# Residuals on TensorE, full-turn row transposes and a partition-aligned split in a decoder kernel

## The reference

```
x = layernorm(x + gated_delta_attention(x))        # stage 1
x = layernorm(x + cross_attention(x, ctx))         # stage 2
x = layernorm(x + quantum_ffn(x))                  # stage 3
x = layernorm(x + selective_scan(x))               # stage 4
x = layernorm(x + perceiver_attention(ctx, x))     # stage 5
x = layernorm(x + receptance_ffn(x))               # stage 6
```

## Time and profile before

| what | value |
|---|---|
| runs of the kernel | 404.0, 406.8, 408.42 us; median 406.8 |
| the profiled execution, its own time | 406.31 us |
| span from first to last instruction | 403.4 us |
| mean granted TensorE clock | 0.954 |
| PE / DVE / ACT / POOL busy | 331.6 / 319.8 / 210.8 / 224.4 us |

### The profile page before, as it was taken

How to read it: one execution, slowest core, us unless ns; L and a number is a source line. 1 busy time by engine, 2 the same in 40 slices (tenths; PEclk the granted TensorE clock), 3 DMA queues, 4 the chain that set the end, 5 groups by cost and what they waited for, 6 DMA issues and landing times. The chain is left out here.

```text
span 403.4 us, 5113 instructions
## 1 busy us (share of the span) xinstructions
PE 331.6 (82%) x1578; PEld 221.6 (55%) x1578; DVE 319.8 (79%) x638; ACT 210.8 (52%) x462; POOL 224.4 (56%) x228
## 2 busy tenths in 40 slices
PE   5538748789788889779997888895899999999991
PEld 2332447787564626332433543352498877898870
DVE  1599999996877798999999899799868544754536
ACT  2642222231255669577777165663456666674650
POOL 3599899993413142779899889995502700100002
PEclk9957959999999989999999999999999999999996
DMA  8900000000000003335444434443200000000001
GB/s 267 382 30 0 0 3 1 2 1 2 0 2 0 0 2 107 95 101 160 143 139 138 150 99 126 122 137 103 61 0 1 2 0 2 1 2 2 0 0 52
DMA packets 11520, 24.52 MB, mean 61 GB/s; under 512 B 1231, under 2 KB 2255, under 8 KB 11239
## 3 DMA queue, kind: packets, MB, share of 16 engines
q1 hardware_dynamic: 11495, 24.22, 19.0%
HBM read 23.63 MB, written 0.59 MB: 60 GB/s over the span
## 5 line engine op out<-in xcount | busy, mean ns | idle before, releaser
L1057 POOL TENSOR_TENSOR arena<-arena 128x512 f32<-128x512 f32 x63 | 79.7, 1278 | 24.7 <-DVE arena L685 23.2
L685 DVE TENSOR_TENSOR_SCAN arena<-arena,ps 128x512 f32<-128x512 f32 x64 | 77.2, 1208 | 0.0
L1736 PE MATMUL ps<-arena,first_in 128*128 128x512 f32 x128 | 66.5, 603 | 5.7 <-POOL arena L1057 5.6
L1349 ACT ACTIVATE arena<-ps,arena 128x248 f32<-128x248 f32 x64 | 29.3, 463 | 41.4 <-DVE arena L716 41.4
L678 DVE TENSOR_TENSOR ps<-arena,ps 128x512 f32<-128x512 f32 x64 | 43.4, 680 | 6.0 <-PE ps L1724 5.4
L1313 ACT ACTIVATE arena<-arena,neg_a 128x508 f32<-128x508 f32 x64 | 43.2, 709 | 9.5 <-DVE arena L685 8.6
L1103 POOL TENSOR_TENSOR rstd<-veps,mhalf 128x4 f32<-128x4 f32 (+2 forms) x6 | 5.2, 860 | 74.4 <-DVE veps L782 68.3
L1570 PE MATMUL ps<-arena,first_in 128*128 128x128 f32 (+1 forms) x256 | 31.7, 286 | 12.8 <-POOL arena L916 12.8
L1570 PEld LDWEIGHTS ps<-arena,first_in 128*128 128x128 f32 x256 | 30.7, 201 | 14.1 <-issue 8.1
L1724 PE MATMUL ps<-arena,pick_wide 96*128 96x512 bf16 x64 | 24.5, 385 | 12.9 <-DVE arena L685 12.8
L1736 PEld LDWEIGHTS ps<-arena,first_in 128*128 128x128 f32 x128 | 23.3, 191 | 20.7 <-POOL arena L1057 12.8
(11 more groups left out here) (285 smaller groups left out, 815.4 us busy)
## 6 DMA issues: line engine op xcount, KB each, us to landing
arena<-c_rows_dram SPq DMA_DIRECT2D x64, 256.0 KB, 3.2
fold_in<-in_fold_dram SPq DMA_DIRECT2D x1, 2056.0 KB, 15.0
late_in<-in_late_dram SPq DMA_DIRECT2D x1, 1422.5 KB, 18.4
early_in<-in_early_dram SPq DMA_DIRECT2D x1, 921.5 KB, 9.3
xres<-in_x_dram SPq DMA_DIRECT2D x1, 512.0 KB, 6.2
rows_in<-in_rows_dram SPq DMA_DIRECT2D x1, 512.0 KB, 15.9
kv_ctx<-in_context_dram SPq DMA_DIRECT2D x1, 480.0 KB, 11.0
first_in<-in_first_dram SPq DMA_DIRECT2D x1, 465.0 KB, 3.8
```

The source lines that it names most:

```text
L685: nc.vector.tensor_tensor_scan(hist[:, q % NBUF], fade[:, q % NFADE], chain(q), 0.0, ALU.mult, ALU.add).then_inc(S("scan"), 1)
L1057: tt(seen[:, q % NBUF], hist[:, q % NBUF], c_wide[:, q % NBUF], ALU.mult).then_inc(S("read_out"), 1)
L1349: act(s5_p[:, u % 2, h], sim_bank(u)[:, h * 256:h * 256 + KV], ACT.Exp, bias=s5_max[:, u % 2, h:h + 1], accum_out=s5_den[:, u % 2, h:h + 1 ...
L1736: mm(y_bank, ident, seen[:, p % NBUF], start=False, stop=p % NS == NS - 1).then_inc(S("seen_used"), 1)
```

## The change

It has three parts, and an order adapted to them.

1. Rows of stage 1: eight full 128x128 transposes into banks 6 and 7 in place of sixteen 64-column matmuls. VectorE's copy takes 64 of the 128 rows over both banks once all eight are done; ScalarE's copy waits for VectorE's.
2. Stages 1 to 3: TensorE first puts the residual into the accumulation bank (`residual_in`, an identity matmul of 512 columns per half), the projection accumulates onto it, and VectorE takes the statistics and the normalization straight from PSUM (`landed`, `normal` with a bank). `add_residual` is left for stage 4 only. Stage 1 projects into banks 2 and 3, and the value rows go to banks 6 and 7. In stage 2 a `residual_in` stands in the place of a `stay_awake(1, 6)` twice. In the loop, `landed(3, 1, 7)` is at q = 0, `normal(3, 1, 7)` at q = 3, `turn_half(3, 1)` at q = 4 (after a wait for `dt_relu`), `columns_out(3, 1)` at q = 5.
3. B's remainder lies on partitions 32 to 63, so that the middle part is stored once: one copy less on VectorE for the first half and one less on ScalarE for the second.

```
         def turned_bank(n, g):
-            return bank(4) if (n, g) == (3, 0) else bank(6 + g)
+            return bank({(1, 0): 4, (1, 1): 5, (3, 0): 4, (3, 1): 6}.get((n, g), 6 + g))
...
-        bc_mid = A(BT // 2).bitcast(BF16)
...
+            def landed(n, g, k):
+
+                ve.wait_ge(S("projected"), (n - 1) * B + (g + 1) * HB)
+                statistics(half(g), landing(g, k))
+                ts(veps[:, g * HB:(g + 1) * HB], mv[:, g * HB:(g + 1) * HB, 1], EPS, None, ALU.add).then_inc(S("var"), 1)
+
+            def landing(g, k):
+
+                rows = bank(k).rearrange("p (b c) -> p b c", b=HB)
+                return {g * HB + i: rows[:, i] for i in range(HB)}
...
-            def normal(n, g):
-                norm_finish(n, g, half(g), xrow[:, n % 2], xrow[:, n % 2])
+            def normal(n, g, k):
+                norm_finish(n, g, half(g), landing(g, k), xrow[:, n % 2])
...
             nc.vector.tensor_copy(ot[:, 0:512].rearrange("p (n i) -> p n i", i=DH),
-                                  bank(6).rearrange("p (i n) -> p n i", i=DH)).then_inc(S("o_rows"), 1)
+                                  bank(6, 2).rearrange("p (i n) -> p n i", i=DH)[:, 0:P // 2]).then_inc(S("o_rows"), 1)
...
-            add_residual(1, 0, bank(6))
-            spread(1, 0)
-            add_residual(1, 1, bank(7))
-            normal(1, 0)
-            spread(1, 1)
+            landed(1, 0, 2)
+            landed(1, 1, 3)
+            normal(1, 0, 2)
             value_rows(0)
             value_rows(1)
-            normal(1, 1)
+            normal(1, 1, 3)
...
-            add_residual(2, 0, bank(2))
-            spread(2, 0)
-            normal(2, 0)
-            add_residual(2, 1, bank(3))
-            spread(2, 1)
-            normal(2, 1)
+            landed(2, 0, 2)
+            normal(2, 0, 2)
+            landed(2, 1, 3)
+            normal(2, 1, 3)
...
-            add_residual(3, 0, bank(0))
-            spread(3, 0)
+            landed(3, 0, 0)
             fraction(3)
-            normal(3, 0)
+            normal(3, 0, 0)
...
-                return tt(bc_r[0:32, cols(g)], bc_f[0:32, cols(g)], bc_parts[0:32, cols(g)], ALU.subtract)
+                return tt(bc_r[32:64, cols(g)], bc_f[0:32, cols(g)], bc_parts[0:32, cols(g)], ALU.subtract)
...
-                tt(bc_parts[64:96, cols(g)], bc_r[0:32, cols(g)], bc_mid[0:32, cols(g)],
+                tt(bc_parts[64:96, cols(g)], bc_r[32:64, cols(g)], bc_parts[32:64, cols(g)],
...
-            step(nc.vector.tensor_copy(bc_parts[32:64, h0], bc_r[0:32, h0]))
-            then(nc.vector.tensor_copy(bc_mid[0:32, h0], bc_r[0:32, h0]))
+            then(nc.vector.tensor_copy(bc_parts[32:64, h0], bc_r[32:64, h0]))
...
                 if q == 0:
-                    add_residual(3, 1, bank(7))
-                if q == 1:
-                    spread(3, 1)
-                if q == 4:
-                    normal(3, 1)
+                    landed(3, 1, 7)
+                if q == 3:
+                    normal(3, 1, 7)
...
+            def residual_in(n, g, k):
+
+                if n == 1:
+                    pe.wait_ge(S("x_in"), 16)
+                else:
+                    pe.wait_ge(S("residual"), 2 * (n - 2) + g + 1)
+                mm(bank(k), ident, xres[:, g * HB:(g + 1) * HB], start=True, stop=False)
+
+            for g in range(2):
+                residual_in(1, g, 2 + g)
             pe.wait_ge(S("osb"), 2)
             pe.wait_ge(S("osb_last"), 1)
-            for g in range(2):
-                for i in range(DH):
-                    mm(bank(6 + g)[:, i * 64:(i + 1) * 64], osb[:, i * T:(i + 1) * T], ident[:, g * 64:(g + 1) * 64],
-                       start=True, stop=True).then_inc(S("o_rows_mm"), 1)
+            for i in range(DH):
+                turn(bank(6, 2)[:, i * P:(i + 1) * P], osb[:, i * T:(i + 1) * T], ident).then_inc(S("o_rows_mm"), 1)
...
-                    mm(bank(6, 2)[:, b * D:(b + 1) * D], otT[:, b * T:(b + 1) * T], W("w_out0"),
-                       start=True, stop=True).then_inc(S("projected"), 1)
+                    mm(bank(2, 2)[:, b * D:(b + 1) * D], otT[:, b * T:(b + 1) * T], W("w_out0"),
+                       start=False, stop=b % HB == HB - 1).then_inc(S("projected"), 1)
...
-            stay_awake(1, 6)
+            pe.wait_ge(S("score0_shift"), 1)
+            residual_in(2, 0, 2)
             turn_probabilities0(0)
...
             turn_probabilities0(1)
-            stay_awake(1, 6)
+            residual_in(2, 1, 3)
...
+            pe.wait_ge(S("gated"), 1)
+            residual_in(3, 0, 0)
             project3(0, 0)
...
+            residual_in(3, 1, 7)
             project3(1, 7)
...
-                if q == 5:
+                if q == 4:
+                    pe.wait_ge(S("dt_relu"), 2)
                     turn_half(3, 1)
```

More of the change, by code:

```diff
@@ L375, in _, with sbuf_rows @@
             tt, stt, ts = nc.vector.tensor_tensor, nc.vector.scalar_tensor_tensor, nc.vector.tensor_scalar
+            def landed(n, g, k):
[5 more added lines that the diff above has]
+                return {g * HB + i: rows[:, i] for i in range(HB)}
             def add_residual(n, g, acc):
                 h = slice(g * HB, (g + 1) * HB)
[L380 to L383 removed]
+                ve.wait_ge(S("residual"), 2 * (n - 2) + g + 1)
                 ve.wait_ge(S("projected"), (n - 1) * B + (g + 1) * HB)
                 then(tt(xrow[:, n % 2, h], acc.rearrange("p (b c) -> p b c", b=HB), xres[:, h], ALU.add))
[L387 to L405 removed]
+            def sbuf_rows(n):
+                return {b: xrow[:, n % 2, b] for b in range(B)}
             def statistics(batches, src):
                 for b in batches:
[L409 removed]
+                    step(nc.vector.bn_stats(stats[:, b], src[b]))
                 join()
@@ L543, in half @@
                 return range(g * HB, (g + 1) * HB)
-            def spread(n, g):
-                statistics(half(g), xrow[:, n % 2])
-                ts(veps[:, g * HB:(g + 1) * HB], mv[:, g * HB:(g + 1) * HB, 1], EPS, None, ALU.add).then_inc(S("var"), 1)
-            def normal(n, g):
-                norm_finish(n, g, half(g), xrow[:, n % 2], xrow[:, n % 2])
+            def normal(n, g, k):
+                norm_finish(n, g, half(g), landing(g, k), xrow[:, n % 2])
             key_rows(0)
@@ L784, in finish5 @@
             def finish5(part):
-                norm_finish(5, part, range(*PARTS[part]), xrow[:, 1], xrow[:, 1])
+                norm_finish(5, part, range(*PARTS[part]), sbuf_rows(1), xrow[:, 1])
             def gated_residual(part):
@@ L798, in variances6 @@
                 first, last = PARTS[part]
-                statistics(range(first, last), xrow[:, 0])
+                statistics(range(first, last), sbuf_rows(0))
                 ts(veps[:, first:last], mv[:, first:last, 1], EPS, None, ALU.add).then_inc(S("var"), 1)
             def finish6(part):
-                norm_finish(6, part, range(*PARTS[part]), xrow[:, 0], xrow[:, 0])
+                norm_finish(6, part, range(*PARTS[part]), sbuf_rows(0), xrow[:, 0])
             for k in range(2, NU):
@@ L1674, in project3 @@
                             ins = mm(bank(k)[:, b % HB * D:(b % HB + 1) * D], s3_act[g][:, f, b % HB * T:(b % HB + 1) * T], w2[:, f],
-                                     start=(f == 0 and b == g * HB), stop=(f == NF - 1 and b == (g + 1) * HB - 1))
+                                     start=False, stop=(f == NF - 1 and b == (g + 1) * HB - 1))
                         if first:
```

41 lines of the change are left out of this document (10 added, 31 removed).

## The result

| | before | changed |
|---|---|---|
| median, us (20 runs each) | 405.75 (403.2 to 410.21) | 402.61 (399.82 to 407.38) |
| profiled execution, us | 406.31 | 402.39 |
| its span | 403.4 | 400.4 |
| mean granted TensorE clock | 0.954 | 0.954 |

The ratio is 0.9918, with a 95% interval of 0.9895 to 0.9941: 0.8% faster. That is inside the 1% that the prediction called hard to tell from no change, but with 20 runs of each kernel the interval leaves out 1. Four runs of the changed kernel, 406.99 to 407.38 us at a mean clock of 0.942 or 0.943, are left out of the ratio; the experiments show where such microseconds go.

A forecast was written before the change was run, and what follows sets the result against it. Handovers between engines bound stages 1 to 3, VectorE the scan loop, nearly all TensorE the chain from 296 us. Terms: -0.2 - 0.5 - 1.3 - 0.7 - 1.25 = -3.95, from 406.3 to 402.4 us; range with rivals 400.8 to 406.4.

The forecast's parts named there:

- stages 1 and 2: Up to stage 3's first VectorE work: no gain at normal(1, 0), then statistics earlier and normalization longer in stage 2; -0.2 us.
- stage 3, first half: add_residual at 138.32 goes with its join (-0.7), the normalization gets 0.2 longer; -0.5 us.
- clock holds: TensorE's granted clock, 0.50 from 144.8 to 148.2 us before, stays at 1.00 through project4; -1.3 us at L658.
- split: Before the first drive: VectorE's copy L663 and its gap go (-0.45), and L650's 0.28 us wait for ScalarE; -0.7 us.
- loop: Scan loop: add_residual goes (-0.7), normalization from PSUM is shorter (-1.2), VectorE idles at q = 3 (+0.65); -1.25 us.
- Nothing hides them: Stage 1: the two residual matmuls ahead of the row turns cost about 1.75 us, nearly all of the 2.7 saved on rows.
- Reading from PSUM: VectorE's reads from PSUM: nothing more for the statistics, 0.05 us more per normalization, 0.2 per half.
- longer than 0.28 us: Sign that the forecast is wrong: VectorE's statistics from PSUM longer than 0.28 us each.
- The rival of a fixed 0.21 per normalization: PSUM has a fixed price, 0.64 us more per half than taken, on five of six halves; 405.6 us, chance 0.07.
- the rival that the loop gives its part back: GpSimd, not the scans, sets when buffers come free; VectorE's 1.25 us turn into waits; 403.7 us, chance 0.15.
- a loop that ends less than 1 us earlier than its first drive does: Sign that the forecast is wrong: loop's end gains less than 1 us beyond its first drive's gain; "its own saving".
- The slower rival: Clock falls in stage 1 and again in stage 2, 1.83 us each on the path; 407.6 us, chance 0.08.

The follow-up runs named there:

- residual later: Changed kernel with stage 1's two residual matmuls moved behind the eight row turns and behind the first four block turns; 404.15 us, 0.9953 of before.
- normalization at q = 4: Changed kernel with the second half's normalization at q = 4 again, its turn and copy one step later; 401.41 us, 0.9894 of before.
- rows alone: Kernel before with only the first part of the change, stage 1's rows by eight full turns; 402.51 us, 0.9893 of before.
- split undone: Changed kernel with B's middle part copied twice again (bc_mid and its second copies back); 404.49 us, 0.9981 of before.
- the first group: The first four follow-up experiments, on one chip with their own runs of the kernel before, 405.78 us.
- rows undone: Changed kernel with stage 1's rows again by sixteen 64-column matmuls, behind the two residual matmuls; 407.48 us, 1.0036 of before.
- before, clock held: Kernel before with ten idle matmuls instead of eight and one behind turn_half(3, 0); 405.15 us, 0.9964 of before.

## Why the prediction was right, and where it was not

Its terms against the two first profiles. Each is read as how much more of the lead has been won at its handover, relative to the `osb` add:

| term | predicted | measured |
|---|---|---|
| before the change's first instruction | 0 | +0.32 |
| stages 1 and 2 | -0.2 | -0.22 |
| stage 3, first half | -0.5 | -0.68 |
| clock holds | -1.3 | -1.36 |
| split | -0.7 | -0.53 |
| loop | -1.25 | -0.53 |
| stages 5 and 6 | 0 | 0.00 |
| outside the span | 0 | -0.92 |
| sum | -3.95 | -3.92 |

The sum agrees because +0.7 in the loop and +0.3 upstream were met by -0.9 outside the span. That time varies from run to run of one kernel: 1.81 to 3.76 us over 75 runs of the kernel before (median 2.5), 1.92 to 2.49 over 32 of the changed one (median 1.98), with no cause found. The profiled execution of the kernel before happened to have 2.91. Only the five middle terms are the forecast's merit: -3.95 forecast, -3.32 found, and 1.36 of these hang on a clock fall in one execution of the kernel before.

**Stages 1 and 2.** `normal(2, 1)` starts 0.47 earlier (32.29 to 31.82) and takes 0.25 longer: -0.22. The step in stage 1 held too: first block turn at 98.21, relative to the `osb` add 0.30 earlier than before, and `normal(1, 0)` 0.13 earlier where the prediction had no gain. "Nothing hides them" was true of the two residual matmuls only where the change puts them; two positions later VectorE's copy hides both, which is the 1.44 us of *residual later*. I had listed what the two matmuls cost and not asked where else they could stand.

**Reading from PSUM.** Four normalizations take 1.36 or 1.37 against 1.11 or 1.12 from SBUF: 0.06 each, where 0.05 was taken. Four statistics take 0.89 against 0.87 (in the same twenty places before the loop 285 ns each against 281; the prediction's sign "longer than 0.28 us" was met by the kernel before already). The rival of a fixed 0.21 per normalization is out. The Trainium skill's "VectorE: DVE Perf Modes", section "The TRN2 errata", has 62 more cycles, by an estimate 65 ns, for every instruction that reads PSUM. On the normalizations that agrees with the runs; on the statistics and on the 512-column products, which show 4 ns and nothing, it does not. It would have made the 24 statistics from PSUM 1.6 us longer, and they are 0.1 longer. Another rule of the Trainium skill, "VectorE: DVE Perf Modes", section "Why PSUM operands drop a tier", fits all of it better: a float32 operand in PSUM keeps VectorE from taking two elements per cycle, which a `tensor_scalar` from SBUF can and a `tensor_tensor` can't. By it, an estimate of 64 cycles (67 ns) per 128 columns and 267 ns per 512, on `tensor_scalar` alone; the rows show 60 and 210. I had cited the section that the runs contradict and passed over the one that explains the rows I used. The runs have the 128-column form only beside the 512-column one of another line, so that the price goes by columns is supported (0.06 and 0.21), not isolated.

**Stage 3.** The add and its join go, as said; `normal(3, 0)` starts 1.00 ahead, and its own lengthening is only 0.10, since it took 1.26 before: 0.90 ahead at its end, 0.68 more than the 0.22 of stage 2.

**The clock.** The mechanism is shown from both sides: holding it in the kernel before gives 1.37 at the softplus product, letting it go in the changed kernel costs 1.6. But "I expect the clock to hold" was stated as a consequence of the change, and that is too much. It held in nine of the ten profiles that have the change's stage 3 and its eight idle matmuls (from `normal(3, 0)` to the softplus product 8.17 or 8.18 us) and fell in the tenth, *normalization at q = 4* (9.18), which is the same code up to the loop. It held in that of *rows alone* as well, whose stage 3 is the kernel before's. The turns of these two, TensorE, *rows alone* and then *normalization at q = 4*:

```profile
141.87 1.19 PE L1526 MATMUL ps<-first_in,xrow 128*128 128x128 f32 x4 [1.10 <-DVE xrow L418]
```

```profile
141.50 1.29 PE L1504 MATMUL ps<-first_in,xrow 128*128 128x128 f32 x4 [0.34 <-DVE xrow L409]
```

The prediction's reason was that `project4` comes closer behind the idle matmuls. With 1.10 us of idle time between them and the turns, as in the kernel before, the clock held; with 0.34, as in the changed kernel, it fell. So this closeness is neither needed for it nor enough, and that the clock held in the profiled execution was in part luck. Whether earlier handovers make holding likelier, the runs don't settle.

**The split.** The copy is worth 0.44 or 0.45. The 0.28 of waiting that was to go as well became 0.21 and not 0: ScalarE was early enough for the softplus product, but its copy of the 32 rows still came 0.21 after VectorE was free. `residual_in(3, 1)` at 149.97 was hidden, as said: the first drive does not wait for TensorE.

**The loop**, the term that failed. By the scan of q = 5 the changed kernel is 0.85 us ahead of its own first drive (12.26 us behind the first scan instead of 13.11), not 1.25. The idle time is 0.80 where 0.65 was forecast (0.87 counted from start to start), the normalization 1.37 where 1.2 was; together they are the missing 0.4. Then 0.35 is given back between the scans of q = 15 and q = 22 and nothing after: -0.86 at q = 15, -0.76 at q = 17, -0.51 at q = 22, -0.53 at the end. The 0.10 is at q = 16, where a drive waits 0.40 instead of 0.31 for TensorE's `widen_b`, which follows GpSimd's product. The 0.25 is at q = 21. VectorE's `b_low` of the second half, changed kernel, and GpSimd's product beside it:

```profile
199.39 0.91 DVE L635 TENSOR_TENSOR arena<-arena 32x512 bf16<-32x512 f32 x1
```

```profile
199.72 1.71 POOL L990 TENSOR_TENSOR arena<-arena 128x512 f32<-128x512 f32 x1
```

and the same instruction in the kernel before and in *split undone*:

```profile
202.62 0.78 DVE L653 TENSOR_TENSOR arena<-arena 32x512 bf16<-32x512 f32 x1
```

```profile
204.31 0.78 DVE L636 TENSOR_TENSOR arena<-arena 32x512 bf16<-32x512 f32 x1
```

In the changed kernel it takes 0.13 longer beside the same GpSimd product, and the scan behind it starts 2.91 us after the one ahead of it instead of 2.65. This 0.25 is the price of the split, the third part of the change: in all ten profiles with B's remainder on partitions 32 to 63 the instruction takes 0.91 or 0.92 us, in the four without it 0.77 or 0.78, and *split undone*, which has the rest of the change, is one of the four (2.66 from scan to scan). In the ten it starts 0.32 or 0.33 us ahead of GpSimd's product, in the four 0.19 or 0.20; how the remainder's new place leads to that, is not shown. So the rival that the loop gives its part back was right for a quarter of the term, by two small shifts and not by GpSimd being the bound: its read-outs still waited for others for 22.0 us in all (24.7 before). The larger loss was the position: at q = 3 VectorE has to wait for `power(3, 1)`, at q = 4 it has not, and that is 1.0 us of loop. The forecast had priced that idle time and not asked whether one step later costs anything. Its own sign against it, a loop that ends less than 1 us earlier than its first drive does, came true: 3.00 against 2.47.

**The slower rival** was mis-sized. The clock does fall in stage 2, near 109 us, in some executions; three profiles of the first group show it. It was priced at 1.83 us a fall, from a 3.4 us stretch; it lasts 10.2 us there and costs 3.96. One such fall alone makes a run of about 407 us, slower than the median of before; the prediction wanted two. By clock and span 5 of the changed kernel's 32 runs seem to have had one (405.0 or more at 0.942 or 0.943; no profile of such a run of this kernel was taken), and the kernel before has such runs too (408.0 to 408.6 at 0.939, 9 of 58 in the first two groups), so between the medians it makes little difference.

**What the gain consists of.** Turning the rows is worth 1.6 to 1.7 us of path (*rows alone*, *rows undone*) where TensorE's own work shrinks by 2.7: VectorE's copy had needed only the first eight of the sixteen matmuls and now needs all eight turns, so it starts 0.90 earlier behind the `osb` add (1.52 instead of 2.42). And the first block turn, which had stood in TensorE's queue behind the second eight matmuls, now waits for the copy alone: it comes 2.27 us behind the `osb` add in *rows alone*, 4.01 before. The residual on TensorE costs 1.5 of that at once (10.04 against 8.54), wins 0.9 back by `normal(3, 0)`, and with the split's 0.44 and the loop's 0.47 the other two parts come to 0.2 us better than none. Taken apart by *split undone* (its 3.96 of clock fall taken off), the residual on TensorE brings the first drive 0.74 later and makes the loop 0.67 shorter, which about cancels, and the split brings the first drive 0.44 earlier and makes the loop 0.2 longer. The prediction had the sizes up to the first drive about right but summed them in the order of the stages, so that it never saw that one part carries the change.

What stays open: the time outside the spans; what decides whether an execution's clock falls at a given place; and how the remainder's place lengthens `b_low`.

## What to carry to other kernels

Cost each part of a change by itself against the kernel before, not only step by step along the path: a part that spends what another gains shows only so. Follow it to the end of the kernel, too: the split saved 0.44 us where it was looked at and cost 0.2 some 45 us later. An instruction added to an engine should be tried two or three positions later, where another engine's copy hides it, and work that waits for a slow helper one step later in the loop. In a chain of handovers with an often idle TensorE, read the granted clock in windows of more than one execution before a microsecond is booked to an edit.

## What the runs showed of the hardware

**The same code can run with a clock fall and without.** Equal instructions, about equally busy before (1.84 and 1.98 us of 3.4), ran at 1.00 once and at 0.50 for 10.2 us another time. Code shifts the odds: the versions with idle matmuls in stage 2 show, by their mean clock, no such fall in 30 runs. What a fall costs differs with the place: 3.9 to 4.0 us in stage 2 (three profiles, 10.2 us of half clock each), 1.0 to 1.8 at 141 to 148 us, 0.9 at 172 to 179 inside the loop (four profiles), and nothing from 271 to 276, where the changed kernel's first profile had one and the rest of the span was still 116.5.

**Full turns are cheap beside thin matmuls.** Eight float32 turns of 128x128 take 1.04 us and leave 8 records; sixteen float32 matmuls of 64 columns over the same data take 3.75 and leave 32, both at full clock and both done nearly back to back.

**A normalization from SBUF waits for GpSimd's product, one from PSUM does not.** The four normalizations in the loop took 2.38 us from SBUF (*rows alone*, as in the earlier trace rows) and 1.37 from PSUM, nearly the 1.36 of stage 1. The second of the four in the kernel before, and GpSimd's product:

```profile
169.49 1.31 DVE L418 TENSOR_SCALAR xrow<-xrow,mv,rstd 128x128 f32<-128x128 f32 x1
```

```profile
169.45 1.26 POOL L1057 TENSOR_TENSOR arena<-arena 128x512 f32<-128x512 f32 x1
```

The four took 320, 1308, 664 and 334 ns: the second ended 0.08 us after this product and the third 0.08 after GpSimd's next instruction, and the profiles of *rows alone* and *before, clock held* show the same. From PSUM all four took 401 to 408 ns, beside a product of GpSimd that ran from 165.16 to 166.44. Reading from PSUM costs 0.25 us per four where GpSimd leaves VectorE alone and saves 1.0 where it does not.
